# Two-layer graph network on one core: partition p holds 64 neighbouring rows instead of every 128th

## The reference

```
h = relu(layernorm(x))
s = adj @ h[:, 0]                                  # sum of one feature over the neighbours
x = x + relu(h @ w_self.T + s * sum(w_neigh, 1))
h = relu(layernorm(x)); Wh = h @ W                 # 4 heads of 64
e = leaky_relu(sl[i] + sr[j]), masked by adj + identity
x = x + elu(softmax(e) @ Wh)
```

## Time and profile before

| | us |
|---|---|
| runs | 1024.81, 1027.20, 1027.91 |
| median | 1027.20 |
| the profiled execution's own time | 1026.31 |
| its span, first to last instruction | 1024.5 |
| busy: TensorE / VectorE / GpSimd / ScalarE | 701.5 / 709.2 / 397.3 / 337.7 |
| queue of SP, share of the 16 DMA engines | 70.7% |

### The profile page before, as it was taken

How to read it: one execution, slowest core, us unless ns; L and a number is a source line. 1 busy time by engine, 2 the same in 40 slices (tenths; PEclk the granted TensorE clock), 3 DMA queues, 4 the chain that set the end, 5 groups by cost and what they waited for, 6 DMA issues and landing times. The chain is left out here.

```text
span 1024.5 us, 13553 instructions
## 1 busy us (share of the span) xinstructions
PE 701.5 (68%) x3025; PEld 464.3 (45%) x3026; DVE 709.2 (69%) x2868; ACT 337.7 (33%) x1481; POOL 397.3 (39%) x458
## 2 busy tenths in 40 slices
PE   1267866878677786768767787776527776777675
PEld 1034433544344443444444444544316665666564
DVE  5657676766766677766766667666237788778876
ACT  1023343343434334343433334334312222322222
POOL 0032323223232323223232232323077777777770
PEclk9978899888998889988898878887658889888878
DMA  9999999999999999999999999991034445545541
GB/s 299 414 422 419 422 422 422 423 425 422 423 420 425 419 418 422 421 405 396 421 422 409 401 415 405 411 407 62 27 106 119 133 128 144 140 133 132 139 127 49
DMA packets 70000, 321.94 MB, mean 314 GB/s; under 512 B 14498, under 2 KB 48721, under 8 KB 53536
## 3 DMA queue, kind: packets, MB, share of 16 engines
q1 hardware_dynamic: 44160, 293.88, 70.7%
q0 software_dynamic: 15360, 17.46, 7.4%
q10 hardware_dynamic: 10400, 9.74, 2.9%
HBM read 312.57 MB, written 17.07 MB: 322 GB/s over the span
## 5 line engine op out<-in xcount | busy, mean ns | idle before, releaser
L690 PE MATMUL p_pack<-big,pack_w 128*128 128x512 fp8e5 x1024 | 305.9, 450 | 165.6 <-DMA big<-in_adj_dram 148.8
L297 POOL DMA_INDIRECT h0g<-h_table,nbr x192 | 191.8, 999 | 473.3 <-ACT nbr L532 387.7
L690 PEld LDWEIGHTS p_pack<-big,pack_w 128*128 128x128 fp8e5 x1024 | 102.9, 106 | 313.7 <-issue 234.6
L917 POOL DMA_INDIRECT big<-row_table,lists x192 | 196.7, 1024 | 82.2 <-issue 56.7
L366 DVE MAX8 tops<-p_pack 128x8 f32<-128x256 f32 x128 | 48.9, 423 | 154.8 <-PE p_pack L690 154.8
L496 ACT ACTIVATE nbr<-keys 128x2 uint32<-128x2 f32 x64 | 13.0, 203 | 363.7 <-DVE keys L401 363.7
L957 PE MATMUL p_u<-big,ident 128*128 128x256 f32 x288 | 95.2, 480 | 51.6 <-DVE big L1086 51.6
L957 PEld LDWEIGHTS p_u<-big,ident 128*128 128x128 f32 x288 | 68.2, 245 | 67.2 <-DVE big L1086 54.8
L655 PE MATMUL p_u<-wselfT,hT 128*128 128x256 f32 x256 | 77.9, 434 | 0.0
L677 PE MATMUL p_row<-w_gat_and_heads,gT 128*128 128x264 f32 x256 | 69.8, 396 | 0.6 <-ACT rows L585 0.6
L1065 DVE TENSOR_TENSOR big<-big,p_pack 128x768 f32<-128x768 f32 x64 | 58.2, 949 | 1.1
(11 more groups left out here) (146 smaller groups left out, 1359.3 us busy)
## 6 DMA issues: line engine op xcount, KB each, us to landing
big<-in_adj_dram SPq DMA_DIRECT2D x128, 2048.0 KB, 18.3
row_table<-rows ACTq DMA_DIRECT2D x64, 132.0 KB, 9.5
big<-row_table SPq DMA_DIRECT2D x32, 264.0 KB, 3.1
x_rows<-in_x_dram SPq DMA_DIRECT2D x8, 1024.0 KB, 12.9
out_dram<-big SPq DMA_DIRECT2D x32, 256.0 KB, 3.1
h0g<-h_table,nbr POOLq DMA_INDIRECT x192, 6.2
big<-row_table,lists POOLq DMA_INDIRECT x192, 2.8
big<-in_L_gnn_w_self_dram ACTq DMA_DIRECT2D x1, 256.0 KB, 4.9
```

Of the source, the lines that this page charges most:

```text
L297: nc.gpsimd.indirect_dma_start(out=h0g[r][:, j:j + 1], out_offset=None, in_=h0_dram[:, :], in_offset=bass.IndirectOffsetOnAxis(ap=nbr[r][: ...
L690: last = nc.tensor.matmul(p_pack[:], pack_w[:, block_no, :], low_bytes(n % HALVES)[:, i, :], start=(block_no == 0), stop=(block_no == BLOC ...
L917: nc.gpsimd.indirect_dma_start(out=dst, out_offset=None, in_=row_dram[:, :], in_offset=bass.IndirectOffsetOnAxis(ap=lists[r][:, a, j:j + 1 ...
```

## The change

Partition p holds rows 64p to 64p+63; row 64p+t lies in partition p of tile t. That holds for `x`, `adj`, `row_table` and the output. A load of half a tile of `adj` is still 128 pieces of 16 KiB, but these lie 64 rows, 2 MiB, apart in DRAM, where they were one row, 32 KiB, apart. A load of eight tiles of `x` is 128 pieces of 8 KiB in place of 1024 pieces of 1 KiB. `h0_columns` is written to the table as it lies, 64 neighbouring values from each partition. The transpose, the copy and their waits go. ScalarE's `sum_neighbours` goes; VectorE adds the three parts itself. The waits on it move to `upd_step` and `u_ready`. GpSimd makes one more constant, `part_no`.

```diff
-    x_tiles = x.rearrange("(t p) d -> p t d", p=P)
+    x_tiles, out_tiles, row_tiles = (a.rearrange("(p t) d -> p t d", p=P) for a in (x, out, row_dram))
+    adj_tiles = adj.rearrange("(p t) m -> p t m", p=P)
...
-                        sp.dma_start(A[n % HALVES], adj[bass.ds(num(k, r) * P, P), s * HALF:(s + 1) * HALF]
+                        sp.dma_start(A[n % HALVES], adj_tiles[:, num(k, r), s * HALF:(s + 1) * HALF]
...
-                nc.gpsimd.iota(rown[:], [[P, TILES]], base=0, channel_multiplier=1,
+                nc.gpsimd.iota(rown[:], [[1, TILES]], base=0, channel_multiplier=TILES,
...
+                nc.gpsimd.iota(part_no[:], [[1, 1]], base=0, channel_multiplier=1,
+                               allow_small_or_imprecise_dtypes=True).then_inc(pool_consts, 1)
...
                     if later_round(k):
-                        wait_alone(pool, s_summed, t - RING + 1)
-                        wait_alone(pool, u_ready, t - RING + 1)
+                        wait_alone(pool, upd_step, (t - RING) * UPD + 1)
                     nc.gpsimd.memset(h0g[r][:, 0:DIRECT], 0.0).then_inc(h0g_clear, 1)
...
-                    step(nc.vector.tensor_scalar(ext_onehot, mcol[:, 0:EXTRA], first_of[r][:], rown[:, 0:1],
+                    step(nc.vector.tensor_scalar(ext_onehot, mcol[:, 0:EXTRA], first_of[r][:], part_no[:],
...
                     wait_alone(dve, u_ready, t + 1)
-                    dve.wait_ge(s_summed, t + 1)
-                    step(nc.vector.tensor_tensor(stot[r][:], svec[r][:], p_first[:, D:D + 1], ALU.add), 1)
+                    dve.wait_ge(h0_in[r], (k + 1) * 16 * OWN)
+                    step(nc.vector.scalar_tensor_tensor(stot[r][:], h0g[r][:, 0:1], h0g[r][:, 1:2], p_first[:, D:D + 1],
+                                                        ALU.add, ALU.add), 1)
...
-                act.wait_ge(h0_turned, 1)
-                nc.scalar.copy(h0r[:], p_cnt[0:TILES, 0:P]).then_inc(h0_copied, 1)
-                act.wait_ge(h0_copied, 1)
-                act.dma_start(h0_dram.rearrange("(t p) o -> t (p o)", p=P), h0r[:]).then_inc(h0_out, 16)
+                act.wait_ge(h0_done, 1)
+                act.dma_start(h0_dram.rearrange("(p t) o -> p (t o)", p=P), h0c[:]).then_inc(h0_out, 16)
...
-                        wait_alone(act, s_summed, t - RING + 1)
+                        wait_alone(act, u_ready, t - RING + 1)
...
-                def sum_neighbours(k, r):
-
-                    t = num(k, r)
-
-                    act.wait_ge(h0_in[r], k * 16 * OWN + 16 * OWN)
-                    if later_round(k):
-                        act.wait_ge(upd_step, (t - RING) * UPD + 1)
-                    nc.scalar.activation(junk[:], h0g[r][:, 0:DIRECT], ACT.Copy, accum_out=svec[r][:]).then_inc(s_summed, 1)
-
...
-                    act.dma_start(row_dram[bass.ds(t * P, P), :], rows[r][:]).then_inc(row_out[r], 16)
-                run(act, (sum_neighbours, 4), (list_neighbours, 1), (count_extras, 1), (keep_maps, 2), (pick_extras, 2),
+                    act.dma_start(row_tiles[:, t, :], rows[r][:]).then_inc(row_out[r], 16)
+                run(act, (list_neighbours, 1), (count_extras, 1), (keep_maps, 2), (pick_extras, 2),
...
-                pe.wait_ge(h0_done, 1)
-                nc.tensor.transpose(p_cnt[0:TILES, 0:P], h0c[:], ident[:]).then_inc(h0_turned, 1)
-                pe.wait_ge(h0_copied, 1)
...
-                    sp.dma_start(G[r][:, :, 0, :], row_dram[bass.ds(t * (2 * P), 2 * P), :].rearrange("(a p) d -> p a d", p=P)
+                    sp.dma_start(G[r][:, :, 0, :], row_tiles[:, two(k, r), :]
...
-                    sp.dma_start(out[bass.ds(t * (2 * P), 2 * P), :].rearrange("(a p) d -> p a d", p=P), res[r]
+                    sp.dma_start(out_tiles[:, two(k, r), :], res[r]
```

More of the change, by code:

```diff
@@ L114, in preln_gnn_gat_kernel @@
         h0c = sb("h0_columns", [P, TILES])
-        h0r = sb("h0_rows", [TILES, P])
         ident = sb("ident", [P, P])
@@ L121, in preln_gnn_gat_kernel @@
         rown = sb("rown", [P, TILES])
+        part_no = sb("part_no", [P, 1])
         wselfT = sb("wselfT", [P, DC, D])
@@ L157, in preln_gnn_gat_kernel @@
         h0g = ring("h0g", [P, OWN])
-        svec = ring("s", [P, 1])
         stot = ring("stot", [P, 1])
-        junk = sb("junk", [P, DIRECT])
         junk1 = sb("junk1", [P, EXTRA])
@@ L188, in preln_gnn_gat_kernel @@
         stat0_done, ln0_step, sd0_done, h0_done = sem("stat0_done"), sem("ln0_step"), sem("sd0_done"), sem("h0_done")
-        h0_turned, h0_copied, h0_out = sem("h0_turned"), sem("h0_copied"), sem("h0_out")
+        h0_out = sem("h0_out")
         w_turned, w_copied, wa_step = sem("w_turned"), sem("w_copied"), sem("wa_step")
@@ L199, in preln_gnn_gat_kernel @@
         h0g_clear = sem("h0g_clear")
-        s_summed = sem("s_summed")
         h0_in = [sem(f"h0_in{i}") for i in range(RING)]
@@ L274, in _ @@
                                allow_small_or_imprecise_dtypes=True).then_inc(pool_consts, 1)
-                pool.wait_ge(pool_consts, 3)
+                nc.gpsimd.iota(part_no[:], [[1, 1]], base=0, channel_multiplier=1,
+                               allow_small_or_imprecise_dtypes=True).then_inc(pool_consts, 1)
+                pool.wait_ge(pool_consts, 4)
                 nc.gpsimd.affine_select(out=ident[:], in_=ident[:], compare_op=ALU.not_equal, fill=1.0,
@@ L280, in _ @@
                 nc.gpsimd.memset(earlier[:], 1.0).then_inc(pool_consts, 1)
-                pool.wait_ge(pool_consts, 5)
+                pool.wait_ge(pool_consts, 6)
                 nc.gpsimd.affine_select(out=earlier[:], in_=earlier[:], compare_op=ALU.is_gt, fill=0.0,
@@ L315, in _ @@
                 nc.vector.memset(ones[:], 1.0).then_inc(consts, 1)
-                dve.wait_ge(pool_consts, 6)
+                dve.wait_ge(pool_consts, 7)
                 for i in range(BLOCKS_IN):
@@ L597, in _ @@
                 pe.wait_ge(w_in, 16 * 5)
-                pe.wait_ge(pool_consts, 6)
+                pe.wait_ge(pool_consts, 7)
                 for i, raw in enumerate((w_raw, wn_raw)):
@@ L722, in each_dense_tile, with of_tile @@
                 eng.wait_ge(tiles_listed, 1)
+        def of_tile(table, t):
+            return table[:, bass.ds(t, 1), :].rearrange("p a d -> p (a d)")
         def x_at(t):
@@ L733, in load @@
                     sp.wait_ge(d_free, i + 1)
-                    sp.dma_start(x_at(t), x[bass.ds(t * P, P), :]).then_inc(d_in, 16)
+                    sp.dma_start(x_at(t), of_tile(x_tiles, t)).then_inc(d_in, 16)
                     for s in range(2):
-                        sp.dma_start(A[s][:, 0:HALF], adj[bass.ds(t * P, P), s * HALF:(s + 1) * HALF]).then_inc(d_in, 16)
+                        sp.dma_start(A[s], of_tile(adj_tiles[:, :, s * HALF:(s + 1) * HALF], t)).then_inc(d_in, 16)
                         sp.dma_start(h0_all[s], h0_dram[s * HALF:(s + 1) * HALF, :].rearrange("n o -> o n")
@@ L752, in _ @@
                 with dve.If(dve.value_load(dense_count[0:1, 0:1], min_val=0, max_val=TILES) > 0):
-                    step(nc.vector.tensor_scalar(tile_no[:], rown[0:1, :], 1.0 / P, 1.0, ALU.mult, ALU.add), 6)
+                    step(nc.vector.tensor_scalar(tile_no[:], rown[0:1, :], 1.0, None, ALU.add), 6)
                     step(nc.vector.tensor_tensor(listed[:], listed2[:], tile_no[:], ALU.mult), 7)
@@ L772, in sums @@
                                                             ALU.mult, ALU.add, part[:, s:s + 1]), s + 1)
-                    step(nc.vector.tensor_tensor(svec[0][:], part[:, 0:1], part[:, 1:2], ALU.add), 3)
+                    step(nc.vector.tensor_tensor(stot[0][:], part[:, 0:1], part[:, 1:2], ALU.add), 3)
                     dve.wait_ge(d_u, i + 1)
-                    step(nc.vector.scalar_tensor_tensor(y[0][:], vsum[:], svec[0][:], p_u[0][:, 0:D], ALU.mult, ALU.add), 4)
+                    step(nc.vector.scalar_tensor_tensor(y[0][:], vsum[:], stot[0][:], p_u[0][:, 0:D], ALU.mult, ALU.add), 4)
                     step(nc.vector.scalar_tensor_tensor(x_at(t), y[0][:], 0.0, x_at(t), ALU.max, ALU.add), 5)
@@ L801, in norms @@
                     act.wait_ge(d_row_copied, i + 1)
-                    act.dma_start(row_dram[bass.ds(t * P, P), :], rows[0][:]).then_inc(d_out, 16)
+                    act.dma_start(of_tile(row_tiles, t), rows[0][:]).then_inc(d_out, 16)
                     act.wait_ge(d_out, (i + 1) * 16)
@@ L1153, in load @@
                     for s in range(2):
-                        sp.dma_start(A[s][:, 0:HALF], adj[bass.ds(t * P, P), s * HALF:(s + 1) * HALF]).then_inc(e_in, 16)
-                    sp.dma_start(e_self, row_dram[bass.ds(t * P, P), :]).then_inc(e_in, 16)
+                        sp.dma_start(A[s], of_tile(adj_tiles[:, :, s * HALF:(s + 1) * HALF], t)).then_inc(e_in, 16)
+                    sp.dma_start(e_self, of_tile(row_tiles, t)).then_inc(e_in, 16)
                     def block_rows(n, s, b):
@@ L1161, in load @@
                     sp.wait_ge(e_res, i + 1)
```

(2 more changed lines are left out.)

## The result

The changed kernel took 1076.95 us, the median of 1072.67, 1076.95 and 1077.96, against 1027.20 before: 1.0501 times the time, 95% interval 1.0470 to 1.0532. **Slower**, as forecast, by 50 us instead of the 181 of the forecast. Repeated on two later occasions the same code took 1046.03 and 1047.19 us beside 1025.8 each time.

The account below looks back on a forecast made before the run. The prediction took the `adj` load to bound the first stage and GpSimd the second. Its terms: 1026.3 - 5.5 (start) - 2.5 (drain) + 189.8 (`adj` rate) = 1208.1 us, range 1012 to 1461.

Parts of the forecast that it names:

- What bounds the kernel: First stage to 690 us: the `adj` load at 417 GB/s, 643.7 us; second stage: GpSimd's indirect transfers, 250 us.
- The rate of the `adj` load: First stage: wider spacing lowers the load from 417 to 322 GB/s, +189.8 us, bounds 417 and 247.
- my middle case: First stage: `adj` load at 348 to 247 GB/s, so 1146 to 1461 us in all; chance 0.42.
- a small slowing: Rival, first stage: `adj` load at 412 down to 348 GB/s, 1030 to 1146 us in all; chance 0.10.
- The start: Load of `x` in 8 KiB pieces: packing begins near 36.5 instead of 42.78 us; term -5.5 us, bounds 0 and -6.5.
- the spacing costs nothing: Rival, first stage: `adj` load stays above 412 GB/s, 1018.3 us in all, between 1012 and 1024, faster; chance 0.30.
- The `h0` table: Start: transpose, copy and waits go, the table is written in 128 pieces of 256 bytes, all covered; zero.
- The sum on VectorE: Zero in the first stage, being covered; in the drain two waits for ScalarE go, -2.5 us, bounds 0 and -4.
- The second stage: Loads, writes and gathers after the drain: unchanged, zero, covered by GpSimd's 250 us.

Follow-up runs that it names:

- e1: The changed kernel with each tile of `adj` again 128 neighbouring rows, 32 KiB apart: 1020.71 us, ratio 0.9931 to the kernel before.
- e2: The kernel before with only the pieces of `adj` moved 2 MiB apart: 1049.91 us, ratio 1.0220.
- f1: The changed kernel unaltered, run again on a later occasion: 1046.03 us, ratio 1.0201 to the kernel before.
- e8: The changed kernel with partition p holding 16 neighbouring rows in each of four groups of 2048, `adj` pieces 512 KiB apart: 1020.53 us, ratio 0.9956 to the kernel before.
- e3: The changed kernel with the pieces of `adj` 63 rows (2016 KiB) apart instead of 64: 1022.72 us, ratio 0.9954 to the kernel before.
- e4: The changed kernel with the pieces of `adj` 16 rows (512 KiB) apart: 1022.76 us, ratio 0.9966 to the kernel before.
- f3: The changed kernel with the pieces of `adj` 48 rows (1.5 MiB) apart: 1021.81 us, ratio 0.9965 to the kernel before.
- e5: The kernel before with `adj` pieces 2 MiB apart and `x` loaded in pieces of 8 KiB: 1047.41 us, ratio 1.0232.
- e6: The changed kernel with `x` loaded in the old pieces of 1 KiB: 1048.45 us, ratio 1.0232 to the kernel before.

## Why the prediction was right or wrong

**What bounds the kernel: right.** The load of `adj` sets the first stage, nothing covers it, and the sign came from there, as e1 and e2 show from both sides. All other engines' shares fell with the stage.

**The rate of the `adj` load: the step that failed, by its size.** I took 322 GB/s "for a size and not for a cause", +189.8 us. It measured 385 (packing +54.2 us) and on later occasions 401 (f1: packing 687.18 us, +25.8). The value came from short pieces of `x`, which is another way of filling the engines without moving much; it bore on this pattern in nothing but having a low number. The bounds, 247 to 417, held the truth and the range held the time, but my middle case, 348 to 247 with 0.42, was the wrong one: what happened I had as "a small slowing", 0.10. The transfers themselves are the nearer rows: 128 pieces of 16 KiB swung between 424 and 401 with nothing changed, and the loss turned out of that order. The Trainium skill's ratio would have given 1214 us, no nearer: its copies, which also write to memory, lost 23% (an estimate from that page), these loads 4 to 8%. That its 320 GB/s and my 322 lay so close was no support for either.

**The start: right in kind, -5.5 forecast.** Packing begins 4.1 us earlier (38.67), not 6.3. The timeline of the changed kernel's start:

```profile
27.45 2.71 DVE L325 BATCH_NORM_STATS2 stat<-x_rows 128x6 f32<-128x256 f32 x8 [0.45 <-DMA x_rows<-in_x_dram]
...
31.43 0.37 ACT L483 COPY w_neigh_sums<-p_u 128x256 f32<-128x256 f32 x1 [2.16 <-PE p_u L599]
31.82 1.28 ACT L486 ACT_TABLE_LOAD   x1
33.11 0.35 ACT L486 ACTIVATE tmp<-tmp,eps 128x64 f32<-128x64 f32 x1
33.57 0.55 DVE L341 RECIPROCAL rstd<-tmp 128x64 f32<-128x64 f32 x1 [2.13 <-ACT tmp L486]
```

The statistics end at 30.2 instead of 35.8, near the 29 forecast. Then VectorE waits 2.13 us for ScalarE's square root, which stands behind the copy of the weight sums, and that is late because the weights are: ScalarE's own loads land later now.

```profile
26.68 1.97 PE L593 MATMUL p_u<-ident,big 128*128 128x128 f32 x8 [26.68 <-DMA big<-in_L_gnn_a_r_dram]
```

And in the kernel before:

```profile
14.18 1.97 PE L603 MATMUL p_u<-ident,big 128*128 128x128 f32 x8 [14.18 <-DMA big<-in_L_gnn_a_r_dram]
```

I had costed the weight loads at nothing and named no cover for them: the new form of the `x` load delayed them by 12.5 us. And of the 4.1 us only part reaches the end: the last packing begins at 702.0 in e1 and e8 and at 700.9 to 702.7 in e3, e4 and f3, 1.5 to 3.3 us before the 704.17 of the earlier trace rows. e1's span is 5.3 us under the kernel before, 2.2 of it by the last packing, 1.9 in the drain and 1.3 in the second stage; its median is 5.6 us under, near the 8.0 forecast for "the spacing costs nothing" (1018.3).

**The `h0` table: right.** GpSimd clears at 45.56 and waits for its first index until 48.88; a table in 512 pieces of 64 bytes (e8) cost nothing to see.

**The sum on VectorE: right in the stage, smaller in the drain.** Late in the stage of the changed kernel:

```profile
751.06 0.21 DVE L453 SCALAR_TENSOR_TENSOR stot<-h0g,p_u 128x1 f32<-128x1 f32 x1
...
753.71 0.12 POOL L293 MEMSET h0g<- 128x2 f32 x1
```

The sum costs 0.21 us instead of 0.15, and the clearing comes 2.4 us after its end, as forecast. In the drain the wait for ScalarE is gone, but one for TensorE has its place:

```profile
772.33 0.28 PE L646 MATMUL p_u<-h0g,map 128*128 128x1 f32 x2
...
772.65 0.21 DVE L453 SCALAR_TENSOR_TENSOR stot<-h0g,p_u 128x1 f32<-128x1 f32 x1 [1.51 <-PE p_u L646]
```

I had named what is late next for no tile but one. From the last packing to the second stage, the three kernels with the sum on ScalarE take 38.5, 38.5 and 36.4 us (before, e2, e5), the eleven with the new sum and unsplit transfers 34.6 to 38.2, mean 36.0: about -1.8 instead of -2.5, with a spread of the same size.

**The second stage: right.** 282.5 against 281.9 us, with 1030 ns for a gather instead of 1024.

## What to carry to other kernels

A stage that is bound by one large load has no cover, so before its rows are dealt out anew, look at the distance between the pieces that one transfer reads: here one row less than 2 MiB, or a grouping that makes it 512 KiB, kept all of the rate. A price taken from a row should resemble the disputed thing in what is being changed, not only in being low. And run the changed kernel itself beside its variants on each occasion: without it, two removals each looked like the cause.

## What the runs showed of the hardware that I had not expected

Loads of 128 pieces of 16 KiB keep 415 GB/s at 63 rows apart and run at 401 or 385 at 64 rows, by occasion, 4 to 8% under the 417 before. The same bytes in transfers of 64 neighbouring partitions run at 223 GB/s, in transfers of 64 alternate partitions at 390 (50 to 690 us). In both, the DMA share of that stretch reads 1.0: it doesn't tell a full pipe from a slow one. And the form of the load on one queue sets the pace of another: with pieces of 8 KiB on SP's queue instead of 1 KiB, ScalarE's last weight load of 128 KB took 23.6 us to land instead of 10.8. The weight loads of the changed kernel and then of the kernel before, us to landing last:

```profile
big<-in_L_gnn_w_self_dram ACTq DMA_DIRECT2D x1, 256.0 KB, 8.4
big<-in_L_gnn_w_neigh_dram ACTq DMA_DIRECT2D x1, 256.0 KB, 13.5
w_gat_and_heads<-in_L_gnn_W_dram ACTq DMA_DIRECT2D x1, 256.0 KB, 18.3
big<-in_L_gnn_a_l_dram ACTq DMA_DIRECT2D x1, 128.0 KB, 20.9
big<-in_L_gnn_a_r_dram ACTq DMA_DIRECT2D x1, 128.0 KB, 23.6
```

```profile
big<-in_L_gnn_w_self_dram ACTq DMA_DIRECT2D x1, 256.0 KB, 4.9
big<-in_L_gnn_w_neigh_dram ACTq DMA_DIRECT2D x1, 256.0 KB, 7.1
w_gat_and_heads<-in_L_gnn_W_dram ACTq DMA_DIRECT2D x1, 256.0 KB, 8.0
big<-in_L_gnn_a_l_dram ACTq DMA_DIRECT2D x1, 128.0 KB, 8.2
big<-in_L_gnn_a_r_dram ACTq DMA_DIRECT2D x1, 128.0 KB, 10.8
```

Each of the five lands later. e5 and e6 show that it is the form of the `x` load. This is the last of the five in e5, the kernel before with pieces of 8 KiB, and then in e6, the changed kernel with pieces of 1 KiB:

```profile
big<-in_L_gnn_a_r_dram ACTq DMA_DIRECT2D x1, 128.0 KB, 24.3
```

```profile
big<-in_L_gnn_a_r_dram ACTq DMA_DIRECT2D x1, 128.0 KB, 10.7
```

Two things change with that form, and no run parts them: the length of the pieces, and how soon they are queued, for SP is done with issuing the eight loads of `x` after 4.0 us in the changed kernel and after 23.2 before. The Trainium skill (DMA: Bandwidth & Descriptors, Queues, rings and completion order) has each DMA engine take turns between queues packet by packet. If longer pieces make longer packets, the other queue waits longer, which would agree; no trace here shows the packets of a turn.
